# Transposing the gated Y and the normalised x by 32 x 32 squares on VectorE and DMA instead of on TensorE

## What is computed

```
xn = layernorm(x)
x + mamba(xn) + ffn(xn)

mamba: x_branch, z = split(xn @ in_proj.T)                 1024 + 1024 features
       x_branch    = silu(causal_conv4(x_branch) + conv_b)
       X, dt, B, C = split(x_branch @ x_proj.T)            16 heads of 64; B, C of 128
       dt          = softplus(dt @ dt_proj.T + dt_bias)
       Y           = ssd(X * dt, -exp(A_log) * dt, B, C) + X * D
       result      = (Y * silu(z)) @ out_proj.T
ffn:   (sigmoid(xn @ q(w1).T) * (xn @ q(w2).T)) @ q(w3).T  q: weights to -1, 0, 1; 1408 hidden
```

## Time and profile before

| | |
|---|---|
| median of 3 runs | 1691.93 us (1691.35 to 1694.18) |
| the profiled execution, its own time | 1692.29 us |
| its span in the profile | 1690.5 us |
| mean granted TensorE clock | 0.981 of 2.4 GHz |
| busy: PE, DVE, ACT, POOL | 1609.1, 1128.3, 914.3, 487.6 us |
| share of the span | 95%, 67%, 54%, 29% |
| DMA | 89.75 MB, 47086 packets, mean 53 GB/s |
| of the packets under 512 B, under 2 KB | 5968, 6736 |

### The profile page before, as it was taken

How to read it: one execution, slowest core, us unless ns; L and a number is a source line. 1 busy time by engine, 2 the same in 40 slices (tenths; PEclk the granted TensorE clock), 3 DMA queues, 4 the chain that set the end, 5 groups by cost and what they waited for, 6 DMA issues and landing times.

```text
span 1690.5 us, 25949 instructions
## 1 busy us (share of the span) xinstructions
PE 1609.1 (95%) x9682; PEld 791.0 (47%) x9682; DVE 1128.3 (67%) x1818; ACT 914.3 (54%) x1871; POOL 487.6 (29%) x469
## 2 busy tenths in 40 slices
PE   6488779999999999999999999999999999999999
PEld 3233334545445544454444454454544544444444
DVE  7767876587556875567756776568855677566762
ACT  6676545466354653556444763556636565356641
POOL 4223212143131440324212441214403243033320
PEclk9798889999999999999999999999999999999999
DMA  6354330111001110011101210012100121002100
GB/s 223 111 164 137 102 111 23 39 54 57 26 7 58 51 44 19 26 58 45 50 1 37 59 57 26 7 46 63 38 26 13 52 62 51 1 26 65 55 8 26
DMA packets 47086, 89.75 MB, mean 53 GB/s; under 512 B 5968, under 2 KB 6736, under 8 KB 46960
## 3 DMA queue, kind: packets, MB, share of 16 engines
q1 hardware_dynamic: 46960, 88.08, 16.8%
HBM read 79.41 MB, written 8.65 MB: 52 GB/s over the span
## 4 chain that ended last, share of the span: by engine, by line
PE 75%; DVE 9%; ACT 8%; issue 5%; DMA 2%; POOL 0%; SPq 0%; DVEq 0%; ACTq 0%; POOLq 0%
PE bank L561 18%; PE bank L473 12%; PE bank L577 9%; PE bank L386 9%; PE bank L402 7%; PE bank L543 7%; PE bank L412 5%; ACT edc L786 4%; PE bank L505 2%; PE bank L517 2%; PE bank L533 1%; PE bank L490 1%; PE bank L425 1%; DVE edc L1116 1%; DVE mdc L1122 1%
## 5 line engine op out<-in xcount | busy, mean ns | idle before, releaser
L473 PE MATMUL bank<-wx_hi,arena 128*128 128x512 f16 x1024 | 321.2, 384 | 0.0
L561 PE MATMUL bank<-xt_hi,q 128*128 128x512 f16 x704 | 268.0, 381 | 1.0 <-ACT q L848 1.0
L561 PE MATMUL bank<-xt_lo,q 128*128 128x512 f16 x704 | 267.8, 380 | 0.0
L1377 POOL TENSOR_TENSOR xst<-xdt,dst 128x512 f32<-128x512 f32 x64 | 66.8, 1043 | 575.4 <-DVE xdt L1070 575.4
L473 PE MATMUL bank<-wx_lo,arena 128*128 128x512 f16 x512 | 197.0, 385 | 0.0
L577 PE MATMUL bank<-q,arena 128*128 128x512 fp8e4 x704 | 162.4, 379 | 0.0
L473 PEld LDWEIGHTS bank<-wx_hi,arena 128*128 128x128 f16 x1024 | 101.4, 99 | 116.1 <-issue 6.6
L786 ACT ACTIVATE edc<-csl,csv 128x128 f32<-128x128 f32 x512 | 155.8, 389 | 0.0
L1116 DVE TENSOR_TENSOR edc<-edc,gt 128x512 f32<-128x512 f32 x128 | 87.9, 727 | 66.4 <-ACT edc L791 66.3
L816 ACT CAST arena<-full 128x512 f16<-128x512 f32 x88 | 54.6, 620 | 138.4 <-DVE full L1171 138.4
L1171 DVE SCALAR_TENSOR_TENSOR full<-tnh,bank 128x512 f32<-128x512 f32 x88 | 60.5, 687 | 102.2 <-PE bank L561 100.6
(11 more groups left out here) (183 smaller groups left out, 3550.0 us busy)
## 6 DMA issues: line engine op xcount, KB each, us to landing
csl<-sums SPq DMA_DIRECT2D x128, 256.0 KB, 3.3
res<-w_ffn SPq DMA_DIRECT2D x41, 256.0 KB, 3.4
res<-x SPq DMA_DIRECT2D x32, 256.0 KB, 3.9
out<-res SPq DMA_DIRECT2D x32, 256.0 KB, 2.0
arena<-w_x SPq DMA_DIRECT2D x8, 640.0 KB, 4.7
yac<-x SPq DMA_DIRECT2D x16, 256.0 KB, 2.7
gate<-x SPq DMA_DIRECT2D x16, 256.0 KB, 3.4
arena<-w_in SPq DMA_DIRECT2D x8, 512.0 KB, 6.5
```

Source lines behind the costliest of these rows:

```text
L473: i = pe.matmul(banks[0][:], act[:, k, c * P:(c + 1) * P], wt[:, k, hf * half:(hf + 1) * half], start=(n == 1), stop=(n == 3 * ki))
L561: i = pe.matmul(banks[2 * (m % 2) + j][:], q12[:, j, k, m * P:(m + 1) * P], part[:, k, :], start=(n == 1), stop=(n == 2 * kd))
L1377: pool.tensor_tensor(by_head(xst[:], hd), by_head(xdt[:], hd), heads_over(sml["dst"][:, c, :], hf * hph, hph, hd), ALU.mult).then_inc(S["x ...
```

## The change

PE turns only the x of block 0 (`turn_first`). Elsewhere a matrix of 128 x 128 is turned in two steps: DVE's `transpose` turns each square of 32 x 32 within itself, and the squares change places on a way through DRAM: the tile is stored row by row, and four DMAs, one for each 32 partitions, fetch it back in runs of 32 floats (128 bytes). For Y this is 8 times a block one store of 256 KB and four loads of 64 KB each (2048 runs in all); it goes through `xs` (under the name `ysq`), which `project_x(u+2)` of ACT therefore rewrites only after `yt_lo(u)`. For x it is, once a block from block 1 on, four stores of 256 KB and four loads of 256 KB (8192 runs in all), in the tiles `mdcs`. ACT and DVE make the high and low parts from there, no longer from the banks.

The order changes with it. `split_y` (the former `turn_y` of ACT and DVE) comes after `decay`; `project_out` comes after `project_z` in the units, and at step 5 of `ffn_up` in place of step 1; the layernorm of the next block is done two pieces at a time in steps 2 to 6 of `ffn_up`; the `x_branch` of the next block begin three steps later in `ffn_down`.

```diff
-FOLLOWING = {(0, 5): 0, (0, 7): 1, (0, 9): 2, (1, 0): 3, (1, 2): 4, (1, 4): 5, (1, 6): 6, (1, 8): 7}
+FOLLOWING = {(0, 8): 0, (0, 10): 1, (1, 0): 2, (1, 2): 3, (1, 4): 4, (1, 6): 5, (1, 8): 6, (1, 10): 7}
...
+        mdcs = sb("mdcs", [P, 4, 2, hpg * P], F16)
+        mdc = [mdcs[:, n] for n in range(4)]
...
+        ysq = xs
+        xsq_all = mdcs[:].rearrange("p n q t -> p (n q t)").bitcast(F32)
+        xsq = [xsq_all[:, k * tb:(k + 1) * tb] for k in range(kd)]
+        x_dram = nc.dram_tensor("x_squares", [chunks, P, dm], F32, kind="Internal").ap()
+        y_dram = nc.dram_tensor("y_squares", [halves, P, half], F32, kind="Internal").ap()
...
+        def squares(dram, j):
+            return dram.rearrange("(i a) (k j b) -> j a k i b", a=SQ, b=SQ, j=P // SQ)[j]
+        def x_squares(j):
+            return x_dram.rearrange("c (i a) (k j b) -> j a k (c i) b", a=SQ, b=SQ, j=P // SQ)[j]
+        def by_feature(t, j):
+            return t[j * SQ:(j + 1) * SQ, :].rearrange("a (k i b) -> a k i b", i=P // SQ, b=SQ)
...
+            def turn_x(b):
+                for c in range(chunks):
+                    sp.wait_ge(S["x_blocks"], at(b - 1, "x_blocks", c))
+                    if c == 0 and b > 1:
+                        sp.wait_ge(D["x_sq_in"], (b - 1) * (P // SQ) * DMA)
+                    sp.dma_start(x_dram[c], xsq[c]).then_inc(D["x_out"], DMA)
+                sp.wait_ge(D["x_out"], b * chunks * DMA)
+                for j in range(P // SQ):
+                    sp.dma_start(xsq_all[j * SQ:(j + 1) * SQ, :].rearrange(
+                        "a (k n b) -> a k n b", k=kd, b=SQ), x_squares(j)).then_inc(D["x_sq_in"], DMA)
+            def turn_y(b, u):
+                hf, n = u % 2, chunks * b + u // 2
+                sp.wait_ge(S["y_blocks"], at(b, "y_blocks", u))
+                if n:
+                    sp.wait_ge(D[f"y_in{hf}"], n * (P // SQ) * DMA)
+                sp.dma_start(y_dram[hf], ysq[hf][:]).then_inc(D[f"y_out{hf}"], DMA)
+                sp.wait_ge(D[f"y_out{hf}"], (n + 1) * DMA)
+                for j in range(P // SQ):
+                    sp.dma_start(by_feature(ysq[hf], j), squares(y_dram[hf], j)).then_inc(
+                        D[f"y_in{hf}"], DMA)
...
                 for u in range(len(units)):
                     if u + 1 < len(units):
                         sums_in(b, u + 1)
+                    if u:
+                        turn_y(b, u - 1)
                     for _ in range(4):
                         aside()
                     if u and u % 2 == 0:
                         load_res(b, u // 2 - 1)
+                turn_y(b, 7)
                 for m in range(kf):
                     if m:
                         aside()
                     if m == 1:
                         load_res(b, 3)
-                    if 1 <= m <= 4 and b < nb - 1:
-                        load_x(b + 1, m - 1)
+                    if m <= 1 and b < nb - 1:
+                        load_x(b + 1, 2 * m)
+                        load_x(b + 1, 2 * m + 1)
+                    if m == 7 and b < nb - 1:
+                        turn_x(b + 1)
...
-            def turn(b):
+            def turn_first():
...
                     pe.wait_ge(S["xt_lo"], at(b, "xt_lo", 3))
+                if b and m == 0:
+                    pe.wait_ge(S["y_added"], at(b - 1, "y_added", 7))
+                elif b and m == 1:
+                    pe.wait_ge(S["yoff"], at(b - 1, "yoff", 7))
+                elif b and m == 2:
+                    pe.wait_ge(S["state"], at(b - 1, "state", 7))
+                elif b and m == 3:
+                    pe.wait_ge(S["attn"], at(b - 1, "attn", 3))
...
-            def turn_y(b, u):
-                if u % 2:
-                    pe.wait_ge(S["yt_lo"], at(b, "yt_lo", u - 1))
-                elif u:
-                    pe.wait_ge(S["attn"], at(b, "attn", u // 2 - 1))
+            def project_out(b, j):
+                pe.wait_ge(S["yt_lo"], at(b, "yt_lo", 2 * j + 1))
+                if j:
+                    pe.wait_ge(S["attn"], at(b, "attn", j - 1))
                 else:
                     pe.wait_ge(S["acc"], at(b, "acc", 7))
-                if b == 0 and u == 2:
+                if b == 0 and j == 1:
                     pe.wait_ge(S["gam"], 1)
-                pe.wait_ge(S["y_gated"], at(b, "y_gated", u))
-                for j in range(per):
-                    i = pe.transpose(banks[7][:, j * P:(j + 1) * P], yac[u % 2][:, j * P:(j + 1) * P],
-                                     idn[:])
-                i.then_inc(S["y_turned"], 1)
-
-            def project_out(b, j):
-                pe.wait_ge(S["yt_lo"], at(b, "yt_lo", 2 * j + 1))
...
                     before_chunk(b, u)
                     aside()
-                    if u:
-                        turn_y(b, u - 1)
                     aside()
                     if u == 0:
...
                         project_x(b, u + 1)
                     update(b, u)
                     aside()
+                    if u + 2 < len(units):
+                        project_z(b, u + 2)
                     if u == 2 and b == 0:
                         pe.wait_ge(S["wout_lo"], ki)
                     if u and u % 2 == 0:
                         project_out(b, u // 2 - 1)
-                    if u + 2 < len(units):
-                        project_z(b, u + 2)
                 if b == 0:
                     pe.wait_ge(S["tern_q"], 2 * pieces_per)
                 for m in range(kf):
                     ffn_up(b, m)
                     if m:
                         aside()
-                    if m == 0:
-                        turn_y(b, 7)
-                    if m == 1:
+                    if m == 5:
                         project_out(b, 3)
-                if b < nb - 1:
-                    turn(b + 1)
...
-                    act.wait_ge(S["x_turned"], at(b, "x_turned", k))
-                    if b and k == 0:
+                    if b == 0:
+                        act.wait_ge(S["x_turned"], k + 1)
+                    elif k == 0:
+                        act.wait_ge(D["x_sq_in"], b * (P // SQ) * DMA)
                         act.wait_ge(S["up_mm"], at(b - 1, "up_mm", 21))
-                    act.copy(xt[0][:, k, :], banks[4 + k][:]).then_inc(S["xt_hi"], 1)
+                    src = xsq[k] if b else banks[4 + k][:]
+                    act.copy(xt[0][:, k, :], src).then_inc(S["xt_hi"], 1)
...
                 if u >= 2:
-                    act.wait_ge(S["y_skip"], at(b, "y_skip", u - 2))
+                    act.wait_ge(S["yt_lo"], at(b, "yt_lo", u - 2))
...
-            def turn_y(b, u):
-                act.wait_ge(S["y_turned"], at(b, "y_turned", u))
-                if u % 2 == 0 and u:
+            def split_y(b, u):
+                hf = u % 2
+                act.wait_ge(D[f"y_in{hf}"], (chunks * b + u // 2 + 1) * (P // SQ) * DMA)
+                if hf == 0 and u:
                     act.wait_ge(S["out_mm"], at(b, "out_mm", u // 2 - 1))
                 elif u == 0 and b:
                     act.wait_ge(S["out_mm"], at(b - 1, "out_mm", 3))
-                hf = u % 2
                 act.mul(yt[0][:, hf * per:(hf + 1) * per, :],
-                        banks[7][:].rearrange("p (k t) -> p k t", k=per), down).then_inc(S["yt_hi"], 1)
...
                     aside()
-                    if u:
-                        turn_y(b, u - 1)
                     if u + 1 < len(units):
                         decay(b, u + 1)
+                    if u:
+                        split_y(b, u - 1)
                     if u == 0:
                         project_z(b, 1)
                     aside()
...
                     ffn_up(b, m)
                     if m:
                         aside()
-                    if m == 0:
-                        turn_y(b, 7)
+                    if m == 3:
+                        split_y(b, 7)
...
+            def squares_of_x(b, c):
+                dve.wait_ge(S["xn"], at(b, "xn", c))
+                dve.wait_ge(S["diag_mm"], at(b - 1, "diag_mm", 12 + c))
+                dve.transpose(xsq[c], xin[c][:]).then_inc(S["x_blocks"], 1)
...
+                dve.wait_ge(S["y_gated"], at(b, "y_gated", u))
+                dve.transpose(ysq[u % 2][:], y_[:]).then_inc(S["y_blocks"], 1)
...
                     before_chunk(b, u)
                     aside()
-                    if u:
-                        turn_y(b, u - 1)
                     if u + 1 < len(units):
                         decay(b, u + 1)
+                    if u:
+                        split_y(b, u - 1)
                     if u == 0:
                         project_z(b, 1)
                     aside()
...
                     if u + 1 < len(units):
                         update(b, u + 1)
                     aside()
-                    if u and u % 2 == 0:
-                        project_out(b, u // 2 - 1)
                     if u + 2 < len(units):
                         project_z(b, u + 2)
```

(61 more changed lines are left out.)

25 lines of the change are left out of this document (8 added, 17 removed).

## The result

The change took **1732.5 us** (median of 4, 1731.8 to 1736.7) against 1691.6 for the kernel before beside it: a ratio of 1.024, interval 1.023 to 1.026. It is slower; 1744 was forecast, with 1664 to 1805.

What follows compares the result with a forecast made beforehand. PE was taken to bound blocks 1 to 7, with DVE full in the units. Terms -12.3 (x transpositions), -16.7 (units), +3 (block 0) and +77.7 (x's stall) gave +51.7: 1744 us, range 1664 to 1805.

Steps and rivals of the forecast that it cites:

- I am wrong if `mdcs` lands within 8 us of its issue: Sign against the forecast of slow x fetches at the seams, whose mdcs loads should land over 15 us after issue.
- +65 on the seams: Seams between blocks: 77.7 us of added stall less 12.3 us of x transpositions taken from PE.
- -14 on the rest: Outside the seam terms: units of blocks 1 to 7 at -16.7 us, block 0 at +3.
- The price of a run: DMA fetches of 128-byte runs: 31 ns each taken, with bounds of 11 and 44 ns.
- rival A: Short runs are cheap: up to 13.3 ns a run x is hidden too, total 1666 us; 27%.
- the stall of x: PE's first x_branch at each of 7 seams: 9.1 us waiting plus 2 of lost clock, +77.7 us in all.
- F + 33.0: Seam: last squares of x ready 33.0 us after F, the start of ffn_up.
- the sum of DVE's circle: Units: DVE's cycle becomes 10.99 + 0.72 = 11.7 us, and the units still gain 16.7 us in 7 blocks.
- The waits that I forecast at the scans of units 1 and 2: Units: PE waits some 0.9 us at unit 1's scan and 1.9 at unit 2's, then DVE catches up.
- Y's way is hidden: Units: Y's way through DRAM needs 7.5 us and 8.4 are covered by other work, so nothing is added.
- Block 0: ACT and DVE set the pace, the preparation of weights beside them: +3 us, between 3.5 gained and 5.8 added.
- rival D: SP's queue stands at Y's store before block 0's weight loads: up to 30 us; 3% that it alone decides (1722).

Runs made afterwards that it cites:

- whole rows: Kernel after, both fetches reading 2 KB rows in place of 128-byte runs, so operands are other numbers (for time alone): 1712.8 us, ratio 1.013.
- earlier squares: Kernel after, all four normalisations and transpositions of x at step 5, ahead of the addition of project_out(3): 1718.0 us, ratio 1.015.
- SP's order in block 0: Kernel after, SP issuing block 0's weight loads ahead of Y's store and between store and fetch: 1722.5 us, ratio 1.019.
- x behind the weights in the first seam: Kernel after, in block 0 alone x's way through DRAM issued behind the last loads of weights: 1726.6 us, ratio 1.020.
- x alone, with its edits: Only x through DRAM, Y turned by PE, squares at step 5, x behind the weights in the first seam: 1685.5 us, ratio 0.996.
- x alone: Kernel before with only x turned by squares through DRAM, Y left on PE: 1700.4 us, ratio 1.006.
- all edits: Kernel after with the four edits (Y's squares, x's squares, SP's order, x behind weights) and two weight pieces in xdt and xst: 1676.9 us, ratio 0.992.

## Why the prediction was right and wrong

The sign and the range were right, but not for the stated reason. By my own sign, "I am wrong if `mdcs` lands within 8 us of its issue", I was wrong: it landed in 5.7. That losses elsewhere came near the sum was luck. The sum put +65 on the seams and -14 on the rest, where the runs show about 0 on the later seams, +26 on block 0 with its seam, and +16 on the units.

1. **The price of a run failed**: "44 - 384 x 0.0345 = 31 ns. I take it." It is 13 ns, near the lower bound of 11 and about the 13.3 up to which rival A had x hidden. I drew a straight line through two sizes and followed it down to a quarter of the smaller one. The 44 ns came from 64 packets of a DMA that was alone in its window, four deep on each engine; 2.8 us of engine time for 1.6 us of window is a poor measure of a price in a long queue. The Trainium skill, "DMA: Bandwidth & Descriptors", section "Why small descriptors are slow (HBM only)", counts cycles, from which I had worked out an estimate of 10 ns. I set it aside because it disagreed with my 512-byte figure by half; by the 13 ns measured it was much nearer than my line.
2. **So the stall of x** is 7.7 us in all, six times, in place of 63, and little clock with it. The rest of that step held to about a microsecond (F + 33.0 was 32.6, the last landing with 13 ns would be 43.4 and was 44.6). The 3.9 us of SP's issuing, which the sum lacks, are the likely reason for the last difference. That the later seams show nothing of PE's saving (6 x 2.19 us) is the short runs again: whole rows bring it back, and so, nearly, do earlier squares.
3. **The units failed in the sum of DVE's circle**, "10.99 + 0.72 = 11.7". The transposition's price was right (0.71). But the circle is no sum of DVE's work. It passes through ACT three times (`edc`, `mdcs`, `xdt_hi`), and an instruction ahead of `xdt` also delays `xdt_hi`, so the 0.70 us for which DVE waits there is not filled by it. And the pair of `edc` instructions grew from 1.37 to 1.85 us, since they now overlap POOL's `yac<-yac,xs`. 10.99 + 0.64 (from one start to the next) + 0.48 = 12.1 of the 12.31; 0.2 is left over. With the transposition behind `xdt` it is 11.61, and the units are 89.4 (forecast 88.7). That meets my 11.7 by luck: there the transposition fills the wait of 0.70 us, and the circle is longer than 10.99 for other reasons, the pair of `edc` at 1.77 us among them. The waits that I forecast at the scans of units 1 and 2, 0.9 and 1.9 us, were 0.95 and 2.38. What the forecast did not have is the 1.26 at the last `project_out`, the fallen clock in five blocks (1.0 each), and some 0.7 in PE's own work: 90.65 less 7 x 0.44 and less the waits of the earlier trace rows is 86.6, where I had added up 85.9. The margin was thin: 24.7 us of PE for two units against 25.1 for the circle, or 23.2 (2 x 11.61).
4. **Y's way is hidden**, as said, in most units: and where the chain went over it (behind unit 6 of block 3, from 856.10 to 863.51) it took 7.4 us from squares to landing, where I had 7.5; two errors cancelled there, a run that was too dear and 2.0 us of SP's issuing that I had left out. With short runs block 0's units were 4.3 us longer than with whole rows, so there it was not all hidden.
5. **Block 0 failed by its order of size**: +3 stands against +18.2 and, behind it, +7.7. I had let ACT and DVE alone set the pace there; the waits show ACT standing for weights, and DVE and PE for ACT. I named the mechanism as rival D, with "up to 30 us", gave it 3% and left it out of the sum. SP's order in block 0 gave back 12.5 of the 18.2, and x behind the weights in the first seam 5.1 of the 7.7. A wait that I had placed in the queue, with a price of up to 30 us, belonged in the sum at half of it or so, not among the rivals.

What stays open: why three later seams of x alone, with its edits, are 0.4 to 0.6 us above the 106.6 of the other three, why block 0's units take 2 us longer with x alone, and which of its waits make up the last 3.5 us of block 0 with all edits. The moves of order that came with the change (`split_y` behind `decay`, `project_out` behind `project_z`) were not tested by themselves; the circle's last 0.2 us may be theirs.

## What to carry to other kernels

Before you put an instruction on an engine that is full, follow the circle through the other engines and find where this engine stands within it: the same 0.71 us a unit cost 20 us more ahead of `xdt` than behind it, where the engine had to wait anyway. A wait put into an in-order queue of DMA issues is paid by everything queued behind it; count what is there and issue it first. A price read from rows of one size holds for that size, so keep both bounds and ask what each rival would need of it.

## What the runs showed of the hardware that I had not expected

- Runs of 128 bytes from DRAM cost about 13 ns of a DMA engine each in a queue of 8192, against 97 ns for 2 KB: a sixteenth of the bytes for a seventh of the time.
- SP's issue of a DMA grows with its runs: in the median 0.32 us for a store of 128 rows, 0.64 for a load of 512 runs (0.42 as whole rows), 1.31 for one of 2048 (0.43 as whole rows). Four of the last took 5.25 us; with whole rows the four took 1.75.
- STREAM_TRANSPOSE of 128x512 f32 on DVE takes 0.711 us, and none of the 92 took over 0.714.
- DVE's TENSOR_TENSOR of f32 slows beside one of POOL. In the kernel after, the 64 of the `edc` group that run beside POOL's `yac<-yac,xs` for over half of their time take 1230 ns in the mean, the 64 with nothing of POOL beside them 683. The group's mean, after:

```profile
L1163 DVE TENSOR_TENSOR edc<-edc,gt 128x512 f32<-128x512 f32 x128 | 117.3, 956 | 64.8 <-ACT edc L828 64.2
```

With x alone, where the two meet less often, the mean is 725 ns.

- A short wait of PE can cost clock. After waits of 0.95 and 2.38 us in two units running, one `project_x` took 6.87 us in place of 5.18. The window (columns as in the earlier trace rows) shows a granted clock of 0.83, so for part of it 1.2 in place of 2.4 GHz. The same two waits in blocks 2 and 3 (568 to 660 and 770 to 861 us) left it at 1.00.

```profile
1393.00:1403.00 10.00, 7.62 (x49) 3.41 (x48) 8.58 (x12) 6.70 (x16) 5.21 (x4) 0.83 0.41 99
```
